# The start of an adaptive-norm block on one core: identity matmuls during the loads, the rest of the modulation one chunk later, constants dealt over the steps

## What is computed

```python
mod = (_silu(L0_c) @ L0_wmod).reshape(8, 6, 1, -1)          # c: 8 x 256, wmod: 256 x 1536
sa, ca, ga, sb, cb, gb = (mod[:, i] for i in range(6))
ga = (2 * (ga >= 0) - 1) * jnp.maximum(jnp.abs(ga), 0.25)   # gates, kept away from zero
gb = (2 * (gb >= 0) - 1) * jnp.maximum(jnp.abs(gb), 0.25)
h = _layernorm(x, axis=-1) * (1 + ca) + sa
x = x + ga * attention(h, w_qkv, w_out)                     # causal linear attention, 16 heads
h = _layernorm(x, axis=-1) * (1 + cb) + sb
x = x + gb * ffn(h, router_w, w1, w2)                       # 8 experts, the 2 best for each row
return x
```

## Time and profile before

| | us |
|---|---|
| median of 3 timed runs (813.83 to 815.63) | 815.24 |
| the profiled execution, as timed | 808.15 |
| its span, first to last instruction | 806.3 |
| VectorE busy in the span | 642.0 (80%) |
| TensorE busy in the span | 717.1 (89%) |
| mean granted clock of TensorE | 0.950 |

### The profile page before, as it was taken

How to read it: one execution, slowest core, us unless ns; L and a number is a source line. 1 busy time by engine, 2 the same in 40 slices (tenths; PEclk the granted TensorE clock), 3 DMA queues, 4 the chain that set the end, 5 groups by cost and what they waited for, 6 DMA issues and landing times.

```text
span 806.3 us, 26650 instructions
## 1 busy us (share of the span) xinstructions
PE 717.1 (89%) x8077; PEld 551.4 (68%) x8077; DVE 642.0 (80%) x1485; ACT 572.9 (71%) x1104; POOL 539.9 (67%) x514
## 2 busy tenths in 40 slices
PE   6589898989898989772599999999999999999994
PEld 3366776767676767661477777777777777777772
DVE  2789999999999999945767787787777787787773
ACT  2478898989898999842067667767767767767762
POOL 4547676767676777733847777777677777777752
PEclk9889999999999999975589999999999999999997
DMA  6313343434343434211123433333433433343320
GB/s 211 88 57 104 100 133 105 130 104 130 104 130 104 130 105 140 67 53 34 42 72 78 73 68 75 70 72 73 79 67 72 80 65 75 77 71 71 77 26 1
DMA packets 52815, 68.80 MB, mean 85 GB/s; under 512 B 8864, under 2 KB 44080, under 8 KB 52736
## 3 DMA queue, kind: packets, MB, share of 16 engines
q0 software_dynamic: 18176, 27.06, 17.7%
q1 hardware_dynamic: 34560, 40.61, 16.4%
HBM read 46.50 MB, written 22.05 MB: 85 GB/s over the span
## 4 chain that ended last, share of the span: by engine, by line
PE 55%; DVE 20%; issue 12%; POOL 8%; ACT 2%; DVEq 1%; DMA 1%; POOLq 0%; SPq 0%; ACTq 0%
PE hidden L1347 16%; PE bank L1365 15%; PE hidden L1349 8%; PE bank L1367 7%; DVE amlo L511 3%; PE bank L1208 3%; DVE w1lo_k L558 2%; PE bank L1191 2%; DVE st L432 1%; POOL mod_b L881 1%; DVE hT L475 1%; POOL rstd L800 1%; POOL qst L840 1%; DVE rb L498 1%; POOL kst L842 1%
## 5 line engine op out<-in xcount | busy, mean ns | idle before, releaser
L1347 PE MATMUL hidden<-qstT,w1hi_k 128*128 128x256 f16 x1136 | 197.9, 274 | 0.7 <-DVE qstT L693 0.7
L1349 PE MATMUL hidden<-qstT,w1lo_k 128*128 128x128 f16 x1136 | 193.6, 220 | 0.0
L1365 PE MATMUL bank<-w,amhi 128*128 x568 | 188.4, 379 | 0.1
L1367 PE MATMUL bank<-w,amlo 128*128 x568 | 154.8, 273 | 0.0
L932 POOL DMA_INDIRECT out_dram<-x,si x71 | 128.7, 1813 | 37.5 <-issue 23.1
L730 DVE TENSOR_TENSOR amlo<-am,amhi 128x512 f16<-128x512 f32 x142 | 98.3, 692 | 49.4 <-ACT am L1079 48.4
L1347 PEld LDWEIGHTS hidden<-qstT,w1hi_k 128*128 x1136 | 111.7, 98 | 13.9 <-issue 0.9
L1349 PEld LDWEIGHTS hidden<-qstT,w1lo_k 128*128 x1136 | 111.7, 98 | 0.2
L1208 PE MATMUL bank<-wq,hT 128*128 128x256 f32 (+1 forms) x256 | 102.8, 527 | 2.3 <-DVE hT L475 2.3
L1365 PEld LDWEIGHTS bank<-w,amhi 128*128 128x128 f16 x568 | 55.6, 98 | 59.9 <-issue 0.4
L808 POOL TENSOR_TENSOR h<-h,mod_b 128x256 f32<-128x256 f32 x64 | 59.7, 933 | 43.4 <-ACT h L954 36.9
(11 more groups left out here) (209 smaller groups left out, 1780.3 us busy)
## 6 DMA issues: line engine op xcount, KB each, us to landing
stage<-in_L_ffn_w_dram SPq DMA_DIRECT2D x32, 512.0 KB, 4.0
xt<-in_L_attn_x_dram SPq DMA_DIRECT2D x32, 128.0 KB, 3.4
out_dram<-x SPq DMA_DIRECT2D x32, 128.0 KB, 3.1
ffn_rows<-h SPq DMA_DIRECT2D x32, 128.0 KB, 1.7
ffn_rows<-am SPq DMA_DIRECT2D x32, 128.0 KB, 3.6
am<-mod_rows SPq DMA_DIRECT2D x16, 128.0 KB, 3.7
mod_b<-mod_rows SPq DMA_DIRECT2D x8, 256.0 KB, 3.7
w<-in_L_wmod_dram SPq DMA_DIRECT2D x6, 256.0 KB, 4.4
```

What stands on the lines that cost most here:

```text
L1347: t.matmul(dst.rearrange("p (q n) -> p q n", q=2), w1s[0][k][g][:, w_], both, start=(k == 0), stop=False)
L1349: last = t.matmul(dst[:, P:2 * P], w1s[1][k][g][:, w_], both[:, 0, :], start=False, stop=(k == KT - 1))
L1365: t.matmul(y[:, :], ghi[:, m.p, c_m], w2s[mt // 2][:, bass.ds(w_, 2 * D)], start=(mt == 0), stop=False)
L1367: last = t.matmul(y[:, D:2 * D], glo[:, m.p, c_m], w2s[mt // 2][:, bass.ds(w_, D)], start=False, stop=(mt == MT - 1))
```

## The change

Five things, all at the start:

1. TensorE multiplies the 128 x 128 fp32 identity with itself into `bank[3]`, which nobody reads: 8 times ahead of the transposes of c, 6 times between them and the first modulation (`keep_awake`).
2. TensorE does the rest of the modulation behind step 1 and not behind step 0, and its wait for GpSimd's constants moves to the end of that.
3. ScalarE, not VectorE, takes the modulation's rows and the router's weights out of PSUM (`rows_of_modulation`, 4 instructions, inside `whi` of chunk 1, so in step 2). `sb` and `cb` are final with that. The gates go into `gates` in SBUF, and VectorE makes them final from there, 5 instructions behind step 2. SyncE's part moves behind step 2 as well, and the scores of chunk 0 wait for ScalarE's four, since they write the same PSUM bank.
4. The gated weights (`wb`) stand one step later in GpSimd's table.
5. GpSimd's constants are dealt out: 6 instructions at once, the masks behind step 0, the sums behind step 1, and the routing's in three parts behind steps 2, 3 and 4.

In the diff, the first `rest_of_modulation` is VectorE's and the second TensorE's; `rows_of_modulation` is ScalarE's.

```diff
-ORDER_POOL = (("rs", 0), ("shk", 2), ("slo", 2), ("wb", 2), ("R", 1), ("xm2", 5), ("h2", 5))
+ORDER_POOL = (("rs", 0), ("shk", 2), ("slo", 2), ("wb", 3), ("R", 1), ("xm2", 5), ("h2", 5))
...
             def rest_of_modulation():
-                dve.wait_ge(s_pe, PE_MOD)
-                link(v.tensor_copy(rw32[:, :, :], rw_ps))
+                dve.wait_ge(s_modr, 4)
                 link(v.tensor_scalar(gate_s, gates, 0.0, 1e30, ALU.is_ge, ALU.mult))
...
-                for q, (k, add) in enumerate((("sb", 0.0), ("cb", 1.0))):
-                    o = MOD[k]
-                    link(v.tensor_scalar(mod_s[o // (4 * D)][:, o % (4 * D):o % (4 * D) + D], rows[:, 1 + q, :],
-                                         add, None, ALU.add))
...
-                "wlo": weights_low}), ORDER_DVE, {1: rest_of_modulation})
+                "wlo": weights_low}), ORDER_DVE, {2: rest_of_modulation})
...
-                "shk": stack_k, "slo": stack_low, "R": rotated, "wb": gated_weights}), ORDER_POOL, {0: attention_constants, 2: routing_constants})
+                "shk": stack_k, "slo": stack_low, "R": rotated, "wb": gated_weights}), ORDER_POOL,
+                    {0: mask_constants, 1: sum_constants, 2: place_constants, 3: row_constants, 4: chunk_constants})
...
+            def rows_of_modulation():
+                act.wait_ge(s_pe, PE_MOD)
+                rows = hidden[1][0:B, :, :].rearrange("p i n -> p (i n)").rearrange("p (q n) -> p q n", n=D)
+                o = MOD["sb"] % (4 * D)
+                copy(gates, rows[:, 0:4:3, :]).then_inc(s_modr, 1)
+                copy(mod_s[0][:, o:o + D], rows[:, 1, :]).then_inc(s_modr, 1)
+                v.activation(mod_s[1][:, 0:D], rows[:, 2, :], ACT.Copy, bias=1.0).then_inc(s_modr, 1)
+                copy(rw32[:, :, :], bank[7][:, 0:KT * E].rearrange("p (k e) -> p k e", k=KT)).then_inc(s_modr, 1)
...
                 copy(piece(m, 0, 1), staged(m, 1), WS).then_inc(a_["whi"], 1)
+                if isinstance(m.n, int) and m.n == 1:
+                    rows_of_modulation()
...
+            def keep_awake(n):
+                for _ in range(n):
+                    t.matmul(bank[3][:, 0:P], ident[:, :], ident[:, :], start=True, stop=True)
             pe.wait_ge(s_pool, POOL_IDENT)
+            keep_awake(8)
             pe.wait_ge(s_ld["c"], 16)
...
+            keep_awake(6)
             pe.wait_ge(s_dve, marks["silu"])
...
             def rest_of_modulation():
-                pe.wait_ge(s_pool, POOL_CONST)
                 pe.wait_ge(s_ld["rw"], 16)
...
                 modulation_of(2).then_inc(s_pe, 1)
+                pe.wait_ge(s_pool, POOL_CONST)
...
+                    if isinstance(m.n, int) and m.n == 0:
+                        pe.wait_ge(s_modr, 4)
...
-                "aT": a_transpose, "pj": projection, "h2T": h2_transpose, "lg": router}), ORDER_PE, {0: rest_of_modulation})
+                "aT": a_transpose, "pj": projection, "h2T": h2_transpose, "lg": router}), ORDER_PE, {1: rest_of_modulation})
...
-                    ORDER_SP, {1: rest_of_modulation})
+                    ORDER_SP, {2: rest_of_modulation})
```

34 lines of the change are left out of this document (18 added, 16 removed).

## The result

| | before | after |
|---|---|---|
| median of 4 timed runs each, same chip | 814.54 (813.59 to 815.63) | 804.47 (803.01 to 805.60) |
| the profiled execution, as timed | 808.15 | 804.04 |
| its span | 806.3 | 802.1 |
| VectorE / TensorE busy in the span | 642.0 / 717.1 | 639.8 / 720.3 |
| mean granted clock of TensorE | 0.950 | 0.953 |

The ratio of after to before is 0.9875, 95% interval 0.9852 to 0.9898, and the medians differ by 10.1 us, where 9.0 were forecast; 804.5 lies in the range of 803.7 to 810.4. The two spans differ by 4.2 us only. So the gain is read from the starts of the same work in both traces and not from the spans.

What follows compares the result with a forecast made beforehand. VectorE, with a beat of 10.1 us a chunk, was taken as the bound. Shifts followed through places A to D put chunk 4's statistics 9.0 us earlier, so 815.24 - 9.0 = 806.2 us, range 803.7 to 810.4.

Steps and rivals of the forecast that it cites:

- Place A: From the start to the end of chunk 0's q and k: products end at 14.1, not 15.86, 1.8 us earlier.
- rival 2: The clock rises but falls before chunk 0's products (5.13 us): 807.2 to 808.7 us, within the forecast's 0.71.
- Rival 1: The identities don't raise the clock: chunk 1's h 3.3 us later, gain 5.7, time 809.5 us; chance 0.17.
- Place B: Chunk 1 without the modulation in between: its transposes 3.6 us earlier, chunk 2's statistics at 19.5, 7.5 earlier.
- Place C: GpSimd in step 2 and the work feeding it: stacking of chunk 1 starts at 32.3, not 40.68, 8.4 us earlier.
- Place D: Gated weights and chunk 4: `wb`'s wait covered by 0.3 us, chunk 4's statistics 8.4 to 9.9 earlier, 9.0 taken.
- rival 4: SyncE loads x for chunk 4 late: if it takes 7 us, gain 7.5, time 807.7; within the forecast's 0.71.

Runs made afterwards that it cites:

- a4: The changed kernel with the gated weights (`wb`) back in step 2 of GpSimd's table: 808.32 us, ratio 0.9986 to the kernel before.
- b1: The changed kernel unaltered, run again on one further chip: 800.57 us against 808.03, ratio 0.9895 to the kernel before.
- b3: The changed kernel with all 13 of the routing's constants in one lump behind step 2: 800.65 us, ratio 0.9895 to the kernel before.
- c3: The changed kernel with VectorE, not ScalarE, taking the modulation's rows out of PSUM: 801.81 us, ratio 0.9923 to the kernel before.
- a2: The changed kernel with its 14 identity matmuls at 8 columns instead of 128: 801.92 us, ratio 0.9912 to the kernel before.
- a1: The changed kernel without its 14 identity matmuls: 800.25 us against 809.35, ratio 0.9895 to the kernel before.
- c1: The changed kernel without identity matmuls and with GpSimd's constants in their two old lumps: 800.76 us against 808.47, ratio 0.9902 to the kernel before.
- c4: The changed kernel with 4 identities ahead of c's transposes, not 8, and 5 and 6 more around chunk 0's later work: 797.75 us, ratio 0.9867 to before.
- a3: The kernel before with the 14 identity matmuls and nothing else: 808.24 us, ratio 0.9995 to the kernel before.
- c2: The kernel before with GpSimd's constants dealt out to steps 0 to 4 and nothing else: 806.51 us, ratio 0.9969 to the kernel before.
- b2: The kernel before unaltered, a single execution on the further chip, run for its trace: 812.29 us.

## Why the prediction was right, step by step

**Place A.** Forecast: c's transposes at 5.1, chunk 0's statistics 1.8 later, products at 11.2 in 2.85, end at 14.1. Measured: 5.32, 2.0 later, 11.35 and 14.2. The identity at 0.44 held: 16 records took 3.78. So did the guess of 2.0 for the modulation at the high level (1.85). But that the clock stayed up was luck. Of the five traces of the changed kernel's 8 and 6 identities it stayed up in two (after, a4); in b1, b3 and c3 it rose and fell again, and the products took 4.54, 5.49 and 4.54. The forecast held rival 2 as a side case; it is at least as common as the main one. Its price at chunk 2 lay between 0.3 and 1.6 (19.34 in after, 19.66 in b1, 20.91 in b3), where 0.9 to 2.5 were given. Rival 1 did not come true, as the identities did raise the clock, but its price of 3.3 was right: a2, where they don't, is 3.1 later than after at chunk 4. What the prediction never worked out is the third case, no identities at all. It booked their delay of c and the clock together. By a1 and c1 their balance at chunk 4 is 0.7 and 0.1 us against after, and no gain in the times. So the step of the forecast that puts a gain of 1.8 us on place A added next to nothing to the result, lucky clock or not.

The Trainium skill (TensorE: Matmul & The Clock Gate, Part 1) says that sustained activity lifts the clock, at a point that moves from run to run. The rises at 5.8, 4.8 and 7.2 us (after, b1, b3) of the same 14 identities agree on the second half. On the first a2 does not: it is busy with hardly a gap from 1.60 to 11.56 and stays at the low level.

**Place B.** Forecast: transposes at 15.9, products at 17.3, chunk 2 at 19.5. Measured: 16.03, 17.41, 19.34. Right to 0.2 us: both are waits taken from rows.

**Place C.** Forecast: exponential of chunk 1 from 28.7 to 29.9, gates to 30.8, chunk 3 at 30.8. Measured: 27.89 to 29.03, 29.73, 29.76. Two terms were too dear. ScalarE's copies were put at 1.5 on the path and cost 0 (c3). They were costed at 1.7 like VectorE's and took 1.2 (24.04 to 25.22), and they ran while the transposed k was not ready; in the sum they held the copy of k up to 25.8, though by its own end of the stacking (24.6) the transposed k could not be there before 25.2; it started at 25.16. The five gate instructions were taken from VectorE's rows with PSUM as a source, 0.68 for 8 x 512. Two of them, with one tensor as input, took 0.41 from SBUF (L414, L417); the third of that size, with two tensors as inputs (L415), took 0.68 as before. So 2.5 and not 3.0. Together chunk 3's statistics were 1.0 earlier than forecast. Little of it went further: the features followed 1.2 behind the statistics and not 0.7, and GpSimd's root stood ahead of the stacking of chunk 1, which started at 32.17, where 32.3 was forecast. The rotation started at 24.41, where 24.6 was forecast.

**Place D.** `wb` waited for nothing (forecast: 0.7), and starts at 35.16, 5.4 behind the end of the gates (5.3 in before). The loads of SyncE were in time, so rival 4 fell. Here the claim that TensorE would keep the high level and have no stretch without work failed. It stood idle for 2.25 us up to 32.83, the clock went down at 33.1 and came back at 39.9, and v of chunk 3 was made at the low level. From the end of the stacking of chunk 1 (35.21) to the exponential of chunk 2 (40.64) it took 5.4, as in before, and not the 3.8 of the sum. The size of the term was right for the high level: c4, which kept it, takes 3.6 (36.05 to 39.68). So the stacking came 8.5 earlier, and the statistics of chunk 4 at 41.17, 8.5 earlier as well, with 40.7 and 9.0 forecast and 8.4 to 9.9 as bounds: the lower bound. A second term that the sum lacked: the rotation fell on VectorE's low halves of the weights, and both became longer, 1.27 to 1.79 on GpSimd and 1.28 to 2.36 on VectorE. In c4 the same overlap stands beside the high level, and chunk 4 follows 0.97 behind the exponential, where it is 0.53 in after: there its price is about 0.4 us, and beside the low level of after none shows.

The Trainium skill (GPSIMD Engine Reference, 1. Specifications) has GpSimd share its SBUF interfaces with VectorE and contend with instructions that have two SBUF inputs. L552 is one, and the trace agrees (2.36 for 1.28, beside the rotation).

**From chunk 4 on.** The claim was that chunk 31 gains as much as chunk 4. It gains 10.9 and not 8.5, for two reasons that the statistics' starts hide. `wb` runs once in a sequence, and in its step the rotation lands on the same work of VectorE. The statistics and low halves in the trace of before, an ordinary step and then the step of `wb`:

```profile
65.94 1.28 DVE L558 SCALAR_TENSOR_TENSOR w1lo_k<-stage,w1hi_k 128x512 f16<-128x512 f32 x2
...
68.84 0.41 DVE L432 BATCH_NORM_STATS2 st<-xt 128x6 f32<-128x256 f32 x1
...
73.87 1.29 POOL L819 TENSOR_TENSOR am<-wo,am 128x512 f32<-128x512 f32 x1
75.10 1.29 POOL L847 TENSOR_TENSOR ra<-ra,rb 128x512 f32<-128x512 f32 x1
...
75.53 2.55 DVE L558 SCALAR_TENSOR_TENSOR w1lo_k<-stage,w1hi_k 128x512 f16<-128x512 f32 x2
...
79.49 0.41 DVE L432 BATCH_NORM_STATS2 st<-xt 128x6 f32<-128x256 f32 x1
```

and the same in after, one step on:

```profile
69.89 0.41 DVE L426 BATCH_NORM_STATS2 st<-xt 128x6 f32<-128x256 f32 x1
...
76.57 2.54 DVE L552 SCALAR_TENSOR_TENSOR w<-stage,w 128x512 f16<-128x512 f32 x2
...
80.53 0.41 DVE L426 BATCH_NORM_STATS2 st<-xt 128x6 f32 x1
```

A step with `wb` takes 10.65 where its neighbours take 9.57. The change sets it one step later, so of the seven such steps between chunks 4 and 31 the last now lies behind chunk 31's statistics: 1.1 of the 10.9 is owed there and is paid before the routing, which starts 9.1 earlier. A further 1.2 comes from the step between the statistics of chunks 7 and 8, which takes 10.8 to 11.0 in before, a3 and c2, although `wb` isn't in it, and 9.57 in a4, the changed kernel with `wb` in its old place. What made it long in before is open. For the sum it means that the pipeline from chunk 4 on is untouched to within 1.2 us, not exactly. That the longer low halves of VectorE are what lengthens the step of `wb` is read from these rows; no run separates them from `wb`'s own 1.3 us on GpSimd.

**The time.** At the routing the first two traces are 9.1 apart, b1 and b2 on the second chip 11.8; the low stretches at the end of the attention stage differ between them, so neither is exact. The medians on the first chip say 10.1, with an interval of 8.3 to 12.1 by the ratio; on the second chip 7.5 (b1), and 8.5 by the ratio, 5.7 to 11.2. So 9.0 was right as far as the runs can tell, and the forecast's own error of half a us at chunk 4 is smaller than that. Two small slips of the forecast change nothing: 5 us of gain make 810.2 and not the 810.4 of the range, and the first four chunks are 9 us over four beats only if the 4.63 us ahead of chunk 0's statistics are counted; from there it is 4.8. The expert stage of after ran unevenly in the first trace: from the first block's output to the last it took 381.4, where before took 378.1 and a1, a3, b1, b2, c2 and c4 377.8 to 378.5, so that its lead sank from 7.5 us to 4.2. b1 is the same program, so it is not the change; what it was stays open. That the time came out near 9.0 holds some luck: chunk 4's 8.5 is made without the gain of place A and without the high clock of place D, and the moved step of `wb` and the step behind chunk 7 add to it later.

**What the parts are worth**, by chunk 4: the move with `wb` 8.4 (c1). Within it 7.5 are lost if `wb` goes back (a4) and 1.9 to 2.05 if VectorE takes the rows (c3); these losses overlap and are not shares of a sum. The identities: 0.1 to 0.7 against after, within the scatter, not visible in the times. The dealing of constants: nothing that shows beside the move (b3, c1), and 1.8 in step 3 of the kernel before (c2).

## What to carry to other kernels

When work is moved back in a pipeline's start, look for the instruction that will wait for its result in an in-order queue, and for what is behind it: here one entry of GpSimd's table left in place would have cost 7.5 of the 8.5 us, and the edits that removed the same wait didn't add up. Price matmuls that only hold the clock up against leaving them out, not only against a lower clock: here they delayed small work that others wait for, and no run shows a gain in time from them. Take the copy of a small PSUM result to the engine that is about to wait, and read the cost of the next reader from a row with its own source.
